# A recurrent mixing kernel on one core: GpSimd adds the bonus terms of the recurrence in VectorE's place, and the middle turns are written out

## The reference

```python
def wkv(w_decay, u, k, v):
    W = -jnp.exp(w_decay)
    ...
    def step(carry, kv_t):
        p, q, o = carry
        kt, vt = kv_t
        no = jnp.maximum(o, u + kt)
        A = jnp.exp(o - no)
        Bc = jnp.exp(u + kt - no)
        y = (A * p + Bc * vt) / (A * q + Bc)
        no2 = jnp.maximum(W + o, kt)
        A2 = jnp.exp(W + o - no2)
        B2 = jnp.exp(kt - no2)
        return ((A2 * p + B2 * vt, A2 * q + B2, no2), y)

def time_mix(x, tmk, tmv, tmr, w_decay, u_first, Wk, Wv, Wr, Wo):
    xx = time_shift(x)
    xk = x * tmk + xx * (1.0 - tmk)
    ...
    sr = jax.nn.sigmoid(xr @ Wr)
    return sr * wkv(w_decay, u_first, k, v) @ Wo

x = x + lif(time_mix(layer_norm(x, ln1_s, ln1_b), ...))
x = x + lif(channel_mix(layer_norm(x, ln2_s, ln2_b), ...))
```

## Time and profile before

| | us |
|---|---|
| time, median of three runs (675.87, 678.21, 679.1) | 678.21 |
| span of the profiled execution, first to last instruction | 675.9 |
| PE busy | 587.6 (87%) |
| DVE busy | 549.4 (81%) |
| ACT busy | 536.8 (79%) |
| POOL busy | 433.9 (64%) |

### The profile page before, as it was taken

The page is one execution under the profiler, slowest core; times in us unless marked ns, Lnnn a source line. Parts: engine busy times, 40 slices in busy tenths (PEclk is TensorE's granted clock), DMA queues, the critical chain, the costliest instruction groups (busy, mean ns, idle before and its releaser), DMA issues. The chain is left out here.

```text
span 675.9 us, 10747 instructions
## 1 busy us (share of the span) xinstructions
PE 587.6 (87%) x2241; PEld 365.2 (54%) x2241; DVE 549.4 (81%) x1532; ACT 536.8 (79%) x849; POOL 433.9 (64%) x576
## 2 busy tenths in 40 slices
PE   1246489999999999999999999999999999989783
PEld 0022146566655656575656665665657565656562
DVE  2865878989898998989898989899898989775631
ACT  4846377988989897979798898989797979857672
POOL 4323554687778685877768777868587774745352
PEclk9858889999999999999999999999999999999996
DMA  6110010001010100001010101010000101000000
GB/s 222 62 32 2 1 32 16 17 17 32 17 32 16 33 16 13 18 16 31 16 31 16 31 16 31 16 31 15 18 17 0 32 2 31 17 1 16 1 16 16
DMA packets 26538, 16.81 MB, mean 25 GB/s; under 512 B 1152, under 2 KB 25728, under 8 KB 26240
## 3 DMA queue, kind: packets, MB, share of 16 engines
q1 hardware_dynamic: 26496, 16.34, 7.9%
HBM read 12.14 MB, written 4.19 MB: 24 GB/s over the span
## 5 line engine op out<-in xcount | busy, mean ns | idle before, releaser
L780 ACT ACTIVATE hid<-p_f,scale 128x512 f32<-128x512 f32 x128 | 87.9, 687 | 64.9 <-PE p_f L1721 64.4
L1721 PE MATMUL p_f<-a_lo,w_hi 128*128 128x512 f32 x320 | 133.2, 416 | 3.0 <-DVE a_lo L293 1.7
L1721 PE MATMUL p_f<-a_hi,w_hi 128*128 128x512 f32 x320 | 125.9, 393 | 0.0
L1721 PE MATMUL p_f<-b_lo,w_hi 128*128 128x512 f32 x256 | 111.9, 437 | 3.6 <-DVE b_lo L293 2.3
L1721 PE MATMUL p_f<-b_hi,w_hi 128*128 128x512 f32 x256 | 100.5, 393 | 0.0
L427 POOL TENSOR_TENSOR rstd<-var,minus_half 128x4 f32<-128x4 f32 x64 | 84.9, 1326 | 2.5
L774 ACT ACTIVATE a_hi<-hid 128x512 fp32r<-128x512 f32 x128 | 79.1, 628 | 3.2 <-DVE hid L1260 1.5
L443 POOL TENSOR_TENSOR nd<-factors,pq 128x512 f32<-128x512 f32 x32 | 39.2, 1224 | 54.6 <-DVE pq L1127 54.5
L293 DVE TENSOR_TENSOR a_lo<-hid,a_hi 128x512 fp32r<-128x512 f32 x96 | 64.5, 696 | 10.5 <-ACT a_hi L774 10.4
L1721 PEld LDWEIGHTS p_f<-a_lo,w_hi 128*128 128x128 f32 x320 | 60.2, 188 | 23.1 <-issue 8.8
L293 POOL TENSOR_TENSOR b_lo<-hid,b_hi 128x512 fp32r<-128x512 f32 x32 | 46.5, 1467 | 39.1 <-ACT b_hi L774 34.7
(11 more groups left out here) (141 smaller groups left out, 1451.2 us busy)
## 6 DMA issues: line engine op xcount, KB each, us to landing
xa<-in_x SPq DMA_DIRECT2D x16, 256.0 KB, 2.8
xb<-in_x SPq DMA_DIRECT2D x16, 256.0 KB, 3.0
out<-y_out SPq DMA_DIRECT2D x16, 256.0 KB, 3.0
kk<-in_ffn SPq DMA_DIRECT2D x1, 1024.0 KB, 6.0
hid<-in_ffn SPq DMA_DIRECT2D x1, 1024.0 KB, 8.4
mix<-in_mix SPq DMA_DIRECT2D x1, 512.0 KB, 6.2
gate<-in_ffn SPq DMA_DIRECT2D x1, 512.0 KB, 4.0
mix<-in_mix SPq DMA_DIRECT2D x1, 320.0 KB, 3.8
```

The source lines that it names most:

```text
L780: act.activation(hid[:, m], p_f[m % 2][:, :], ACT.Gelu, scale=scale[:, 1 + layer, m:m + 1]).then_inc(s_gelu[layer], 1)
L1721: last = pe.matmul(out_, w[:, b], x[:, k], start=(k == 0 and t == 0), stop=(k == n - 1 and t == len(terms) - 1))
```

## The change

GpSimd takes over the two additions: `denominator` and `numerator` become steps of its queue, the first between its two products and the second behind them, in all three kinds of turn. They are gone from VectorE's orders; VectorE's `terms` for n = 0 now also waits until the numerator of the group before has been formed. Second, the loop is gone: `schedule` calls `turn` for the turns 6 to 13 too, with a flag `edge` that is false there, so that TensorE's additional waits stay away from just these turns. All group numbers are now plain numbers.

```diff
 class Group:
-    def __init__(self, pair, step):
+    def __init__(self, pair, step, edge=True):
         self.n = 2 * pair + step
         self.par = step % 2
         self.turn = pair + step // 2
+        self.edge = edge
...
-            loop = range(6, GROUPS - 2)
             for i in range(first, last + 1):
-                if i == loop[0]:
-                    with fori(loop[0] // 2, len(loop) // 2 + loop[0] // 2) as pair:
-                        turn(groups(pair, 0), on(6))
-                        turn(groups(pair, 1), on(7))
-                elif i not in loop:
-                    which = first_turn if i < 3 else turn if i < GROUPS else last_turn
-                    which(groups(i // 2, i % 2), on(i))
+                which = first_turn if i < 3 else turn if i < GROUPS else last_turn
+                which(groups(i // 2, i % 2, not 6 <= i < GROUPS - 2), on(i))
...
+            def denominator(g):
+
+                pool.wait_ge(s_expB, g.n + 1)
+                pool.wait_ge(s_apq, 2 * g.n + 1)
+                pool.tensor_tensor(nd[:, 1], nd[:, 1], factors[:, 2], ALU.add).then_inc(s_den, 1)
+
+            def numerator(g):
+
+                pool.wait_ge(s_bv[0], g.n + 1)
+                pool.wait_ge(s_apq, 2 * g.n + 2)
+                pool.tensor_tensor(nd[:, 0], nd[:, 0], bv[:, 0], ALU.add).then_inc(s_num, 1)
...
                 if on[1]:
                     weighted_sum(g[1], 1)
+                    denominator(g[1])
                     weighted_sum(g[1], 0)
+                    numerator(g[1])
...
                 dve.wait_ge(s_expB, g.n + 1)
                 dve.wait_ge(s_v, g.n + 1)
+                if n == 0:
+                    wait(dve, s_num, g.n)
...
-            def denominator(g):
-                dve.wait_ge(s_expB, g.n + 1)
-                dve.wait_ge(s_apq, 2 * g.n + 1)
-                dve.tensor_tensor(nd[:, 1], nd[:, 1], factors[:, 2], ALU.add).then_inc(s_den, 1)
-
-            def numerator(g):
-                dve.wait_ge(s_bv[0], g.n + 1)
-                dve.wait_ge(s_apq, 2 * g.n + 2)
-                dve.tensor_tensor(nd[:, 0], nd[:, 0], bv[:, 0], ALU.add).then_inc(s_num, 1)
-
...
                     terms(g[1], 1)
-                    denominator(g[1])
                     sum_over_time(g[1], 0)
                     terms(g[1], 0)
                 if on[4]:
                     stats_5(g[4])
-                if on[1]:
-                    numerator(g[1])
                 if on[4]:
                     moments_5(g[4])
...
-                    if isinstance(g.n, int):
+                    if g.edge:
                         after(pe, s_f0_lo, g.n - 3)
```

More of the change, by code:

```diff
@@ L50, in __init__ @@
         self.turn = pair + step // 2
+        self.edge = edge
 def after(eng, sem, n, per=1, nth=1):
[L55 to L59, removed]
+    if n < 0:
+        return
+    if n >= GROUPS_IN_ALL:
+        n, nth = GROUPS_IN_ALL - 1, per
     eng.wait_ge(sem, per * n + nth)
 def wait(eng, sem, count):
-    if not isinstance(count, int) or count > 0:
+    if count > 0:
         eng.wait_ge(sem, count)
@@ L309, in build, with schedule, groups @@
         block = ctx.enter_context(nc.Block())
-        def schedule(fori, first_turn, turn, last_turn, first=-2, last=GROUPS + 3):
+        def schedule(first_turn, turn, last_turn, first=-2, last=GROUPS + 3):
             def on(i):
                 return {k: 0 <= i - k < GROUPS for k in range(-2, 5)}
-            def groups(pair, step):
-                return {k: Group(pair, step - k) for k in range(-2, 5)}
-            loop = range(6, GROUPS - 2)
+            def groups(pair, step, edge):
+                return {k: Group(pair, step - k, edge) for k in range(-2, 5)}
             for i in range(first, last + 1):
-                if i == loop[0]:
-                    with fori(loop[0] // 2, len(loop) // 2 + loop[0] // 2) as pair:
-                        turn(groups(pair, 0), on(6))
-                        turn(groups(pair, 1), on(7))
-                elif i not in loop:
-                    which = first_turn if i < 3 else turn if i < GROUPS else last_turn
-                    which(groups(i // 2, i % 2), on(i))
+                which = first_turn if i < 3 else turn if i < GROUPS else last_turn
+                which(groups(i // 2, i % 2, not 6 <= i < GROUPS - 2), on(i))
         @block.sync
@@ L361, in turn @@
             def turn(g, on):
-                if not isinstance(g[0].n, int) or 1 <= g[0].n < GROUPS - 2:
+                if 1 <= g[0].n < GROUPS - 2:
                     load_a(g[-2])
-                if on[0] and (not isinstance(g[0].n, int) or g[0].n > 0):
+                if on[0] and g[0].n > 0:
                     load_b(g[0])
@@ L634, in last_turn @@
                     shift_2(g[1])
-            schedule(pool.Fori, first_turn, turn, last_turn)
+            schedule(first_turn, turn, last_turn)
         @block.scalar
@@ L741, in relu @@
                 wait(act, s_fv, g.n)
-                if isinstance(g.n, int) and g.n == 0:
+                if g.n == 0:
                     act.wait_ge(s_rest[0], 1)
@@ L1004, in last_turn @@
                     inverse(g[1])
-            schedule(act.Fori, first_turn, turn, last_turn)
+            schedule(first_turn, turn, last_turn)
         @block.vector
@@ L1510, in last_turn @@
                     stats_5(g[4])
-                if on[1]:
-                    numerator(g[1])
                 if on[4]:
                     moments_5(g[4])
-            schedule(dve.Fori, first_turn, turn, last_turn)
+            schedule(first_turn, turn, last_turn)
         @block.tensor
@@ L2063, in last_turn @@
                         turn_5(g[4])
-                schedule(pe.Fori, first_turn, turn, last_turn, **turns)
+                schedule(first_turn, turn, last_turn, **turns)
             program(False, last=2)
```

76 lines of the change are left out of this document (38 added, 38 removed).

## The result

The changed kernel takes 698.99 us (median of four runs, 698.53 to 700.58) against 678.54 for the kernel before (four runs): a ratio of 1.031, 95% interval 1.0286 to 1.0334, or 20.4 us. Forecast were 688.5 (680 to 698). The direction was right, the loss twice as large, just outside the range. The profiled execution took 699.42 with a span of 697.3 us.

What follows compares the result with a forecast made beforehand. Turns were a relay of TensorE, then ScalarE, whose logarithm waits for the denominator. Losses of 7.9, 0.9, 0.5 and 0.9 for unrolling make 10.2 us on 675.9: 686.1, or 688.5 as a median; range 680 to 698.

Steps and rivals of the forecast that it cites:

- The logarithm as the place: End of a turn on ScalarE: a denominator delayed beyond 0.18 to 0.47 us makes the logarithm, and so the turn, late.
- The denominator, 0.66 us a turn: GpSimd's denominator addition makes ScalarE's logarithm 0.73 late in turn 12, 0.59 in turn 11; 12 x 0.66 = 7.9 us.
- the in-between case: VectorE's first scan of p holds GpSimd's addition, the second does not: mean 0.66 us a turn; chance 0.36.
- the `b_lo` row: Earlier trace: GpSimd's b_lo, started into VectorE's b_lo, took 1.73 instead of 1.29 us, ending 1.14 after VectorE's end.
- The hold alone: VectorE's scan blocking GpSimd's denominator addition through shared SBUF ports; without any hold the logarithm was put 0.2 us late.
- the small turns: Turns outside 4 to 15: turn 3 without slack, 0.9 us; turns 1, 2 and 16, 0.5 us by estimate.
- The removal at nothing: VectorE's tail loses two additions, about 1.2 us, which only become idle time before the first swiglu; no gain counted.
- Writing out, 0.9 us: Middle turns 6 to 13 unrolled: eight turns at the pace of the already written-out turns 14 and 15, 0.9 us slower.
- A collision with VectorE's old numerator falls away there, so I cost this at nothing too.: GpSimd's queue behind the numerator slips 0.8 us against TensorE's 0.5 us slack for a_lo; cost nothing, otherwise 0.3 a turn.
- The cover: The vanished collision with VectorE's old numerator, expected to absorb GpSimd's queue slip before TensorE needs a_lo.
- The rival that named this mechanism: GpSimd late for TensorE: the slip reaches a_lo, 0.3 us a turn, 3.6 in all, 692.1; chance 0.09.
- The profiled 675.9 as the fastest of the three runs: Base of the sum: profiled 675.9 us taken as the fastest run, with the three runs' median 2.3 higher.

## Why the prediction was right in its direction and wrong in its size

- *The logarithm as the place.* Right. It waits at the end of the turns 2 to 15, 14 times. In turn 3 its wait grew from 0.95 to 1.89 us; the 0.94 more stands against a forecast of 0.9.
- *The denominator, 0.66 us a turn, by the in-between case.* Right in kind: the addition ends 1.06 us after the first scan (442.37 against 440.62 + 0.69) where the `b_lo` row had given 1.14, and the second scan pays. The hold alone, which the forecast put at 0.46 (0.66 less the 0.2 without it), is 0.30, and the addition's length costs 0.48 instead of 0.2. The two are off in opposite directions, so that the sum came near is partly luck. Measured 0.78 to 0.82 a turn, 10.2 us in all against 9.3 with the small turns.
- *The removal at nothing.* Right. VectorE stands 1.00 us ahead of the first swiglu; forecast were over 1.5, since I had not counted that its scans would be held too.
- *Writing out, 0.9 us.* Right: 1.3 to 1.7, and with the additions in place it made no difference that shows (698.27 with the loop). The Trainium skill's advice to unroll (Runtime: NRT & Kernel Launch, "Instruction fetch mechanics") bought nothing here.
- *"A collision with VectorE's old numerator falls away there, so I cost this at nothing too."* This is the step that failed. The cover came: `x1` took 1.75 us instead of 2.27. But the queue, now later, met VectorE's ratio at `var` and lost 0.44 of the 0.52 again. That the slip then measured 0.84 us (6.88 - 6.04) where 0.8 was forecast is in part luck, and it holds for the one turn that was read; against the loop's other turn it is 1.64. It used up TensorE's 0.5 us, made its product 0.49 us late, and pushed GpSimd's `a_lo` into VectorE's pair, 0.65 us longer; TensorE's products behind the pair came 0.66 late, and the turn went from 37.55 to 38.20. In all the numerator costs 698.99 - 690.38 = 8.6 us of the 10.5 by which the forecast was short; an earlier `a_lo` gave back 4.6 to 6.3. The rival that named this mechanism priced it at 0.3 us a turn, slip minus slack, without the collision behind it, and held it for unlikely (0.09).
- *What stays open.* The filling of the stages up to turn 4 was 3.25 us longer than before. 0.94 of it is the logarithm of turn 3; the rest isn't ascribed, since the same stretch was already 1.9 longer in the kernel that is only written out (98.78 against 96.90). The 0.18 us a turn that the numerator costs with `a_lo` early lie in VectorE's pair of `a_lo`; why GpSimd's work beside it (`x1` in one run, `f_out` in the other) stretches it there by 0.2 was not tested.
- *The profiled 675.9 as the fastest of the three runs.* This reading, in the table of the kernel before and in the sum, is wrong, but did no harm. The execution of 675.87 us has a span of 673.7; in all executions the time lies some 2 us above the span. So the profiled one, with a span of 675.9, took some 678 (an estimate), and the 2.3 us that the sum adds for the median stand for this difference.

## What to carry to other kernels

Work moved to another engine delays everything queued behind it there. Follow that queue to the next result that a third engine reads, ask at every step whom the late instruction now meets, and subtract the slack only then: here the meeting cost more than the waiting. Test the parts of a change one by one, since one half can be worse than the whole, and give every rearrangement its own control: two of three places for `x1` that looked harmless cost 14 and 21 us by themselves.

## What the runs showed of the hardware

- With the numerator alone on GpSimd, TensorE waited 1.93 to 2.09 us in ten turns. Behind seven of these waits its granted clock fell to 0.50, the lower of its two levels (1.2 and 2.4 GHz), for some 3.5 us of work; behind three it stayed at 1.00. A slow stretch cost 1.6 us, nearly as much as the wait. Behind waits of 0.26 to 0.35 us (changed kernel) the windows of the turns 4 to 15 all show 1.00.
- A tenth or two of a microsecond decided which engine was held: VectorE's `b_lo` 0.09 us ahead of GpSimd's took 0.68, 0.21 us behind it 1.64.
- Between two scans of VectorE in a row GpSimd's addition did get in, in all of the turns 4 to 15: it took 1.56 to 1.58 us, and the pair 2.30 or 2.31 instead of 1.26.
